# A masked linear layer and a mixture of experts: the transposing transfer of a block's rows, issued in two parts

## The reference

```python
def reference(data, weight, mask, W_gate, b_gate, W_e, b_e):     # data (4, 512, 1024) fp32
    x = data
    w_masked = weight * elem_mask                                # 32x32 blocks of weight kept or dropped
    x = x + einsum('bsk,nk->bsn', layernorm(x), w_masked)
    h = layernorm(x)
    logits = h @ W_gate + b_gate                                 # 8 experts
    top_idx = top_k(logits, 2)
    y_all = relu(einsum('bsd,edh->bseh', h, W_e) + b_e)          # W_e (8, 1024, 1024)
    x = x + mean over the two chosen experts of y_all
    return x
```

## Time and profile before

| | us |
|---|---|
| median of 3 runs | 646.36 (646.34 to 661.23) |
| profiled execution | 645.14 |
| its span, first to last instruction | 643.4 |
| PE busy | 625.6 (97%) |
| DVE busy | 366.7 (57%) |
| ACT busy | 355.0 (55%) |
| POOL busy | 273.1 (42%) |
| DMA: moved, mean rate | 140.25 MB, 218 GB/s |

### The profile page before, as it was taken

The page is one execution under the profiler, slowest core; times in us unless marked ns, Lnnn a source line. Parts: engine busy times, 40 slices in busy tenths (PEclk is TensorE's granted clock), DMA queues, the critical chain, the costliest instruction groups (busy, mean ns, idle before and its releaser), DMA issues.

```text
span 643.4 us, 11277 instructions
## 1 busy us (share of the span) xinstructions
PE 625.6 (97%) x3495; PEld 506.9 (79%) x3498; DVE 366.7 (57%) x647; ACT 355.0 (55%) x434; POOL 273.1 (42%) x252
## 2 busy tenths in 40 slices
PE   6999999999999999999999999999999999999994
PEld 4666777788788878888888888888888877888883
DVE  5896597887977673454346146024333242399842
ACT  7777764766775633535444443543446437365663
POOL 2013212323655246464545255445534435455624
PEclk9999999999999999999999999999999999999996
DMA  8992874589866358979969869768979999966540
GB/s 346 408 406 85 326 281 178 187 328 332 283 247 227 131 193 222 258 184 233 256 181 238 210 194 225 175 167 212 267 206 209 272 202 218 240 110 111 94 75 2
DMA packets 89207, 140.25 MB, mean 218 GB/s; under 512 B 58304, under 2 KB 58304, under 8 KB 89152
## 3 DMA queue, kind: packets, MB, share of 16 engines
q1 hardware_dynamic: 25776, 92.85, 40.3%
q0 software_dynamic: 11376, 33.57, 23.6%
q10 hardware_dynamic: 52000, 13.11, 12.4%
HBM read 87.59 MB, written 46.14 MB: 208 GB/s over the span
## 4 chain that ended last, share of the span: by engine, by line
PE 89%; ACTq 4%; ACT 3%; DMA 2%; issue 1%; SPq 0%; POOLq 0%; DVE 0%
PE psO L577 77%; ACTq L1215 3%; PE psT L869 2%; PE psT L577 2%; PE psT L610 2%; ACT x2T L1224 2%; PE psO L610 1%; PE psG L683 1%; DMA xb<-data_t 1%; DMA turned_odd<-x 1%; PE psS L664 1%; ACT xb L1264 1%; PE psT L651 0%; PE psO L953 0%; PE psT L953 0%
## 5 line engine op out<-in xcount | busy, mean ns | idle before, releaser
L577 PE MATMUL psO<-slots,xT 128*128 (+1 forms) x1728 | 398.1, 391 | 1.5 <-ACT psO L1168 1.3
L577 PEld LDWEIGHTS psO<-slots,xT 128*128 128x128 f32 x1728 | 322.7, 188 | 69.8 <-issue 3.3
L1589 DVE CAST slots<-raw 128x1024 fp32r<-128x1024 f32 x56 | 47.4, 846 | 190.8 <-DMA raw<-L_ffn_W_e 110.0
L577 PE MATMUL psO<-wT,xT 128*128 128x512 f32 x624 | 152.3, 397 | 0.0
L577 PEld LDWEIGHTS psO<-wT,xT 128*128 128x128 f32 x624 | 114.3, 188 | 25.1 <-issue 2.7
L1264 ACT ACTIVATE xb<-psO 128x512 f32<-128x512 f32 x72 | 42.9, 596 | 161.7 <-PE psO L577 119.9
L2016 POOL DMA_INDIRECT rows_out<-xb,tok_of x33 | 59.2, 1794 | 156.9 <-ACT xb L1264 125.3
L2010 POOL TENSOR_TENSOR xT<-x2T,xT 128x1024 fp32r<-128x1024 f32 x35 | 90.4, 2582 | 25.5 <-ACT xT L1232 14.9
L1591 DVE TENSOR_TENSOR slots<-raw,slots 128x1024 fp32r<-128x1024 f32 x56 | 75.0, 1340 | 1.9
L1168 ACT ACTIVATE psO<-bias_slot 128x512 f32 (+1 forms) x72 | 43.4, 602 | 39.1 <-issue 17.9
L1936 POOL TENSOR_SCALAR rs<-squares 128x1 f32<-128x1 f32 x16 | 7.8, 486 | 69.8 <-ACT rows_a L1017 40.6
(11 more groups left out here) (297 smaller groups left out, 639.8 us busy)
## 6 DMA issues: line engine op xcount, KB each, us to landing
raw<-L_ffn_W_e SPq DMA_DIRECT2D x56, 512.0 KB, 5.9
x_rows<-x SPq DMA_DIRECT2D x16, 512.0 KB, 4.6
xb<-data_t SPq DMA_DIRECT2D x12, 512.0 KB, 4.5
mask_stage<-mask_blocks SPq DMA_DIRECT2D x8, 512.0 KB, 10.5
w_stage<-weight_t SPq DMA_DIRECT2D x8, 512.0 KB, 11.2
row_stage<-L_attn_weight SPq DMA_DIRECT2D x8, 512.0 KB, 11.8
xr<-L_attn_data SPq DMA_DIRECT2D x8, 512.0 KB, 6.2
x_planes<-planes_even SPq DMA_DIRECT2D x8, 512.0 KB, 3.0
```

What stands on the lines that cost most here:

```text
L577: last = eng.matmul(psum, xT[:, p, a, kt, :], moving(b, kt), start=(i == 0 and kt == 0 and not seeded), stop=(i == len(PASSES) - 1 and kt ...
L1589: eng.tensor_copy(slots[:, e % 2, HI, kt, :], raw[:, kt % 2, :]).then_inc(c_split, 1)
```

## The change

The transfer of 128 rows by 2048 columns becomes two of 1024 columns. The first writes the transposed high halves (`turned[:, 0:KT, :]`), the second the low halves. The first is issued where the whole one was, behind `seed_half(b+1, 0)`, and adds to a new pair of semaphores, `l_turn_first`. The second, `turn_rest`, is issued behind `seed_half(b+1, 1)` and adds to `l_turn`, on which POOL and SP go on waiting with the same numbers. `join_rows` waits for both. For the last block the two are issued one behind the other.

```diff
-        l_turn = even_odd("l_turn")
+        l_turn, l_turn_first = even_odd("l_turn"), even_odd("l_turn_first")
...
+        def landed_first(b):
+            k = turns_of_dma(b)
+            return l_turn_first[k % 2], 16 * ((k + 1) // 2)
...
-                eng.dma_start_transpose(turned_by(b), rows_of(b).bitcast(U16)).then_inc(l_turn[k % 2], 16)
+                eng.dma_start_transpose(turned_by(b)[:, 0:KT, :], rows_of(b).bitcast(U16)[:, 0:D]).then_inc(l_turn_first[k % 2], 16)
+
+            def turn_rest(b):
+                eng.dma_start_transpose(turned_by(b)[:, KT:, :], rows_of(b).bitcast(U16)[:, D:]).then_inc(l_turn[turns_of_dma(b) % 2], 16)
 
             def join_rows(b):
+                eng.wait_ge(*landed_first(b))
                 eng.wait_ge(*landed(b))
...
                     if n == 0 and b + 3 < N_BLOCKS and by_dma(b + 3):
                         turn_rows(b + 3)
+                    if n == 1 and b + 3 < N_BLOCKS and by_dma(b + 3):
+                        turn_rest(b + 3)
...
             join_rows(SURE)
             turn_rows(LAST)
+            turn_rest(LAST)
             join_rows(SURE + 1)
```

## The result

The changed kernel was first measured at a median of 661.51 us in three executions (655.88, 661.51, 667.72), where the kernel before had 646.36 (646.34 to 661.23): a ratio of 1.0196, 95% interval 1.0134 to 1.0259. The forecast was 646.6, with a range of 644.6 to 652.0; the time lies outside it, and for a reason that the range wasn't built for.

A forecast was written before the change was run, and what follows sets the result against it. PE (TensorE) was taken to bound the kernel, with at most 1.3 us to win in the expert blocks. 645.14 - 0.4 + 0.2 + 0.1 + 0.3 = 645.3, or 646.6 on the median of 646.36; range 644.6 to 652.0.

The forecast's parts named there:

- Step (1): On ACT's queue, a half-size issue takes 0.84 us, two take 1.67, adding 0.33 a block (bounds 0 and +1.34).
- Step (2): Long issues on ACT are backlog; three blocks change by -0.4 us, PE's 1.28 wait becoming 0.9 (bounds -1.3, +2.6).
- rival C: In the expert blocks all of PE's wait goes and nothing comes back: -1.3 us, about 645.1; chance 0.12.
- Step (3): SP's loads and POOL's gather wait for the later second part, costing PE +0.2 and +0.1 us.
- The step's own signs of being wrong: For the later landing: PE waits for L2010, or ACT's seed for L1591, by more than 1 us.
- Step (4): At the kernel's end, ACT is 0.71 us later, costing +0.3 (bounds 0 and 2.2).
- Rival A: On ACT's queue each part's issue waits like the whole: +18.0 us, about 664; chance 0.08.
- Rival B: The last expert's loads or the gathers come past their slack: +2 to +6 us, about 650; chance 0.12.
- Rival D: Backlog moves between seeds, PE waits as before; within 1 us of the forecast, sharing its chance of 0.68.

The follow-up runs named there:

- after_d: The changed kernel, unchanged, run again; its profiled execution took 644.44 us.
- after_b: The changed kernel, unchanged, run again: 646.69 us, ratio 1.001; its profiled execution took 653.22.
- after_pace_first: The changed kernel with SP's weight loads held for the landing of the first part instead of the second: 651.99 us, ratio 1.0026.
- before_lo_first: The kernel before, uncut, with POOL's low part ahead of its gather: 675.5 us, ratio 1.0374.
- after_c: One of two late repeats of the changed kernel, unchanged; the medians of the two were 645.90 and 645.44 us.
- whole_late: The kernel before with the uncut transfer issued behind the second seed instead of the first: 659.64 us, ratio 1.0036.
- before_few_adds: The kernel before, uncut, with the adding scatters bounded to rows 0 to 7 from the third block on: 642.86 us, ratio 0.9949.
- after_few_adds: The changed kernel with the adding scatters bounded to rows 0 to 7 from the third block on: 647.31 us.

## Why the prediction went wrong

**Step (1), the issue.** Mis-sized: 0.84 was forecast, 1.25 measured, 50 times. It lies inside the bounds (0.67 to 1.34) but at the end that the text named as its own refutation ("1.2 or more"). The 0.33 of a plain load was the wrong neighbour: the issue of a transposing transfer nearly doesn't shrink with its columns. Two parts cost 2.50 where the whole cost 1.34 at least.

**Step (2), the backlog.** The cut with the copies between the parts drains it: no wait for a seed between 460 and 622 in `after_d`, so rival C's term (-1.3) and not the -0.4. The claim that nothing above 1.3 us could be won was too strict as well: five halves began late, not one, and the stretch is 2.6 shorter. The row of a wait gives its idle time alone, and short ones have no row.

**Step (3), the later landing.** This is the step that failed. It let only those queues be late that wait for the second part, and took the longest landing of one profiled execution, 10.7 us, for the longest there is; so it had bounds of 0 to 4.8 and 0 to 4.1 (and its 7.2 us of SP's waits left out 3.1 more, for odd turns) where PE lost 9.8 and 1.9, and 2.1 more by the slow clock. POOL's path was right: its gather stood for the second part, and the low part behind it held PE for the 1.9. SP's was not. The bias load that cost the 9.8 was issued at 547.66, 3 us ahead of the second part, and no later in the stretch than before (545.57, where the stretch began 2.7 earlier): it wasn't held back, it was in flight with the part and landed late as the part did. A line of the kernel before shows the place, DVE's last split, that waits for the bias and not for the weights that the prediction followed:

```profile
554.02 0.69 DVE L1589 CAST slots<-raw 128x1024 fp32r<-128x1024 f32 x1 [2.01 <-DMA bias_slot<-L_ffn_b_e]
```

Two more paths aren't in the step at all: PE's own wait for gathered rows (5.2 in `after_b`, 3.8 in `after_pace_first`), and ACT's issue that waits for a late gather (behind the 9.7 in `before_lo_first`). The step's own signs of being wrong are both met in the long execution. As to the size, landings of 13.9 to 23.8 us stand in five of the nine profiles over 650; the other four give no landing of the parts in question. Landings of 12 to 17 stand in undisturbed executions too (`after_c`, `after_d`), where nothing came to wait for them. And the step put the stall down to the change alone, while 26 of 102 executions of the kernel before are over 650 as well. None of these was profiled; that they have the same cause is taken over from `whole_late`, `before_lo_first` and `before_few_adds`.

**The spread of before.** The three times given of the kernel before held the clue: 646.34, 646.36 and 661.23. The upper one is 2.3% above the others, and no term of the sum and no rival was made for it. The range took 0.5 for the spread between runs. A rival "the execution is one of the long ones, in either kernel" with a chance of about a third would have reached to 661 and beyond, and would have said at once that three executions can't separate these kernels. The forecast of 646.6 is near the 646.25 of all 45 executions, and in part by luck: in `after_d` the terms (2) and (4) are -2.6 and +2.2 instead of -0.4 and +0.3, and nearly cancel.

**Step (4), the end.** Forecast +0.3, bounds 0 to 2.2; measured +1.9, or +2.2 with the new wait of 0.32. It is the term (1) again: two issues of 1.25 without cover, and 1.25 ahead of the join.

**Rival A** (each part waits like the whole, about 664) gave the nearest time and by chance only. Its test, first and second part together over 5.5 us in several blocks running, isn't met: in the long execution one second part took 8.72, the median is 1.25. **Rival B** (about 650) has the right place and a price too small. **Rival D** (the cut does nothing) is nearest to the later result, by another way: -2.6 in the blocks and +2.2 at the end. The rule of the Trainium skill, "DMA: Bandwidth & Descriptors", section of rules for kernel authors, that many small transfers be merged into a large one agrees with the issue's price here, 2.50 us for two parts against 1.34; the times of the executions do not show it.

**What stays open.** Why all three of the first executions were long. At the share seen later, 14 of 42, three in a row would come about once in 27 (1/3 to the third power), so chance is not excluded, and nor is a chip on which it is more frequent. Whether the change makes long executions somewhat more frequent (17 of 45 against 26 of 102) is not settled by these counts. Why a packet takes ten times as long during a late landing was not seen.

## What to carry to other kernels

Where some executions of a kernel are long, predict and compare their share as a quantity of its own; a median of three can be of either kind. Bound a hidden transfer by what its landing does beside all other traffic, not by the longest landing of one execution, and count everything that is in flight with it, not only what waits for it. To find what makes it late, look for an edit that makes it happen every time, and take the suspects away under that edit. Do not count on cutting a transposing transfer to halve what its issue costs the queue: only what stands between the parts can pay for the cut.

## What the runs showed of the hardware

A transposing issue of 128 rows takes 1.25 us for 1024 columns and 1.34 for 2048 when nothing hinders it, and a landing 3.0 and 4.3. Per byte these transfers are dear in this kernel, and so is a scatter that adds. The queues of `after_b` in 260 to 620 (packets, MB, share of 16 engines; q0 holds gathers and scatters, q1 the loads, q10 the transposing transfers), and q0 of `after_few_adds` under it:

```profile
q0 software_dynamic: 9360, 29.52, 40.9%
q1 hardware_dynamic: 8064, 29.36, 25.0%
q10 hardware_dynamic: 49053, 12.18, 23.6%
```

```profile
q0 software_dynamic: 9504, 13.93, 13.6%
```

The 12.2 MB of q10, in 49053 packets, take nearly as much of the engines' time as the 29.4 MB of loads, and bounding the scatters takes 15.6 MB and two thirds of q0's share away. The shares count a packet's time as it ran beside the others, so part of this price is the crowding itself. In the long execution the engines were full from 554 on (share over 1.1) and still full at 28 to 57 GB/s from 562 to 570; what landed late in such stretches was the transposing part, a bias load or a gather of rows, whichever was in flight.
